# Local attention: one tile's values sent to their key blocks in two column halves instead of at once

## The reference, cut to what matters

```
w = WINDOW                                   # 32
bq = q.reshape(b, h, nw, w, d)               # 16 heads, d = 64
bk2, bv2 = (look(bk), look(bv))              # a block of 32 queries sees its own
                                             # 32 keys and the 32 before them
sim = jnp.einsum('bhwie,bhwje->bhwij', bq, bk2) * QK_SCALE
attn = jax.nn.softmax(sim, -1)
out = jnp.einsum('bhwij,bhwje->bhwie', attn, bv2)
return out.reshape(b, h, n, d)               # then out @ Wo
```

## Time and profile before

| | |
|---|---|
| median of three runs | 5192.34 us |
| the profiled execution: its time | 5198.14 us |
| its span | 5196.3 us, so 1.84 us lie around it |
| busy | PE 4459.6 us (86%), DVE 3876.7 (75%), ACT 3326.2 (64%), POOL 2834.6 (55%) |
| mean granted TensorE clock | 0.934 |
| mean DMA rate | 65 GB/s |
| `f_vw<-f_vt` transfers | 576 of 128 KB and 384 of 64 KB in the `f` stack for lines 833 to 837, as many in `g` |

### The profile page before, as it was taken

How to read it: one execution, slowest core, us unless ns; L and a number is a source line. 1 busy time by engine, 2 the same in 40 slices (tenths; PEclk the granted TensorE clock), 3 DMA queues, 4 the chain that set the end, 5 groups by cost and what they waited for, 6 DMA issues and landing times. The chain is left out here.

```text
span 5196.3 us, 198441 instructions
## 1 busy us (share of the span) xinstructions
PE 4459.6 (86%) x70382; PEld 2776.0 (53%) x70382; DVE 3876.7 (75%) x8099; ACT 3326.2 (64%) x11398; POOL 2834.6 (55%) x2110
## 2 busy tenths in 40 slices
PE   5999999598897988989889756988989889798896
PEld 1333332266565665656656534665656656566565
DVE  7888787387786877868768545877868778687785
ACT  1777777476585775857758413766757667476584
POOL 3000000376675766757667404766757667576674
PEclk6999999899998999999999876999989999899998
DMA  0000000233233232332332302233333322323233
GB/s 13 1 2 2 2 1 1 76 78 86 73 79 87 74 85 76 78 90 73 86 78 78 84 14 86 77 86 78 79 82 79 86 73 77 87 77 85 73 79 97
DMA packets 415347, 340.20 MB, mean 65 GB/s; under 512 B 170607, under 2 KB 312469, under 8 KB 412693
## 3 DMA queue, kind: packets, MB, share of 16 engines
q1 hardware_dynamic: 413972, 332.35, 24.1%
q10 hardware_dynamic: 768, 0.02, 0.0%
HBM read 100.42 MB, written 30.41 MB: 25 GB/s over the span
## 5 line engine op out<-in xcount | busy, mean ns | idle before, releaser
L946 POOL TENSOR_TENSOR g_rn<-g_ss,g_minus_half 128x8 f32<-128x8 f32 x378 | 718.6, 1901 | 394.9 <-DVE g_ss L1151 392.7
L946 POOL TENSOR_TENSOR f_rn<-f_ss,f_minus_half 128x8 f32<-128x8 f32 x378 | 718.3, 1900 | 388.8 <-DVE f_ss L1151 384.3
L427 DVE TENSOR_REDUCE a_maxima<-a_max 128x1 f32<-128x512 f32 x1024 | 651.5, 685 | 150.2 <-PE a_max L541 144.0
L351 ACT ACTIVATE a_pex<-a_scores 128x512 f32<-128x512 f32 x1024 | 531.9, 607 | 162.9 <-PE a_scores L550 162.9
L1014 ACT ACTIVATE f_ex<-f_bank,f_nmx 128x64 f32<-128x64 f32 x1536 | 461.3, 314 | 137.6 <-DVE f_nmx L1144 136.8
L1014 ACT ACTIVATE g_ex<-g_bank,g_nmx 128x64 f32<-128x64 f32 x1536 | 461.4, 314 | 132.2 <-DVE g_nmx L1144 131.4
L951 POOL TENSOR_TENSOR g_qr<-g_t 128x512 f32<-128x512 f32 x384 | 493.3, 1285 | 11.8 <-DVE g_t L1124 11.8
L951 POOL TENSOR_TENSOR f_qr<-f_t 128x512 f32<-128x512 f32 x384 | 492.1, 1282 | 13.0 <-DVE f_t L1124 13.0
L1254 PE MATMUL g_bank<-g_wqkv,g_xT 128*128 128x512 f32 x744 | 437.5, 673 | 69.5 <-DVE g_qh L1138 49.7
L1254 PE MATMUL f_bank<-f_wqkv,f_xT 128*128 128x512 f32 x744 | 431.9, 665 | 71.9 <-DVE f_qh L1138 51.8
L282 POOL COPY a_v_head<-a_v_all 128x128 f32 (+1 forms) x16 | 4.6, 289 | 697.9 <-PE a_sums L559 697.9
(11 more groups left out here) (252 smaller groups left out, 11214.6 us busy)
## 6 DMA issues: line engine op xcount, KB each, us to landing
f_vw<-f_vt SPq DMA_DIRECT2D x576, 128.0 KB
g_vw<-g_vt SPq DMA_DIRECT2D x576, 128.0 KB
f_vw<-f_vt SPq DMA_DIRECT2D x384, 64.0 KB
g_vw<-g_vt SPq DMA_DIRECT2D x384, 64.0 KB
f_wqkv<-in_f_Wqkv_dram SPq DMA_DIRECT2D x7, 1536.0 KB, 8.1
g_wqkv<-in_f_Wqkv_dram SPq DMA_DIRECT2D x7, 1536.0 KB, 7.8
f_xs<-xf SPq DMA_DIRECT2D x196, 32.0 KB, 1.8
g_xs<-xf SPq DMA_DIRECT2D x196, 32.0 KB, 1.8
```

The source lines that it names most:

```text
L351: act.activation(pex[:, kt % 2, i % NG, :], ps_s[i % 3][:], ACT.Exp).then_inc(act_ex, 1)
L427: dve.tensor_reduce(maxima[:, m // 4, m % 4:m % 4 + 1], ps_max[m % 3][:], AX.X, ALU.max).then_inc(dv_max, 1)
L946: pool.tensor_tensor(rn[:, b, :], ss[:, b, :], minus_half[:], ALU.pow).then_inc(pl_rn, 1)
```

## The change

The ten transfers of a tile become twenty, each of half the columns (256 instead of 512 in every row), in two halves h = 0 and 1. The first ten wait for the first copy of the values and for the sums of groups 0 and 1 that last read the buffer, the last ten for the second copy and groups 2 and 3. Each half has a semaphore of its own; ACT's copy c waits for half c of the tile before, and PE's sums wait for half 0 at group 0 and for half 1 at group 2.

```diff
-        ld_vw = [sem(f"ld_vw{p}", 160 * NT // 2, 160) for p in range(2)]
+        ld_vw = [[sem(f"ld_vw{p}{h}", 160 * NT // 2, 160) for h in range(2)] for p in range(2)]
...
-                    sp.wait_ge(act_v, upto(act_v, L, 2 * t - 1)).then_inc(own["sp"], 1)
-                    sp.wait_ge(pe_o, upto(pe_o, L, 4 * t - 9))
                     p = 1 - q
-                    for jj in range(2):
-                        k, cols = KEYS * jj, slice(512 * jj, 512 * jj + 512)
-                        last, mine = (k, k + WINDOW) if p else (k + BLK, k)
-                        sp.dma_start(vw[last:last + WINDOW, p, 0, :], vt[P - WINDOW:P, 1 - p, cols]).then_inc(ld_vw[p], 16)
-                        sp.dma_start(vw[mine:mine + BLK, p, 0, :], vt[0:BLK, p, cols]).then_inc(ld_vw[p], 16)
-                        for blk in range(1, NB):
-                            r = BLK * blk - WINDOW
-                            sp.dma_start(vw[k:k + KEYS, p, blk, :], vt[r:r + KEYS, p, cols]).then_inc(ld_vw[p], 16)
+                    for h in range(2):
+                        sp.wait_ge(act_v, upto(act_v, L, 2 * t - 2 + h)).then_inc(own["sp"], 1)
+                        sp.wait_ge(pe_o, upto(pe_o, L, 4 * t - 11 + 2 * h))
+                        to = slice(256 * h, 256 * h + 256)
+                        for jj in range(2):
+                            k, cols = KEYS * jj, slice(512 * jj + 256 * h, 512 * jj + 256 * h + 256)
+                            last, mine = (k, k + WINDOW) if p else (k + BLK, k)
+                            sp.dma_start(vw[last:last + WINDOW, p, 0, to], vt[P - WINDOW:P, 1 - p, cols]).then_inc(ld_vw[p][h], 16)
+                            sp.dma_start(vw[mine:mine + BLK, p, 0, to], vt[0:BLK, p, cols]).then_inc(ld_vw[p][h], 16)
+                            for blk in range(1, NB):
+                                r = BLK * blk - WINDOW
+                                sp.dma_start(vw[k:k + KEYS, p, blk, to], vt[r:r + KEYS, p, cols]).then_inc(ld_vw[p][h], 16)
...
-                        act.wait_ge(ld_vw[1 - q], upto(ld_vw[1 - q], L, (t - 1) >> 1, 160))
+                        act.wait_ge(ld_vw[1 - q][c], upto(ld_vw[1 - q][c], L, (t - 1) >> 1, 160))
...
-                        if g == 0:
-                            pe.wait_ge(ld_vw[p], upto(ld_vw[p], L, tj >> 1, 160))
+                        if g % 2 == 0:
+                            pe.wait_ge(ld_vw[p][g // 2], upto(ld_vw[p][g // 2], L, tj >> 1, 160))
```

More of the change, by code:

```diff
@@ L799, in _ @@
         def _(sp):
-            for s in (st_a, st_f, ld_vw[0], ld_vw[1]):
+            for s in (st_a, st_f, *ld_vw[0], *ld_vw[1]):
                 sp.sem_inc(s, ahead[s.num])
```

## The result

The changed kernel takes 5329.67 us (median of four runs, 5324.98 to 5344.12); beside it on the same chip the kernel before takes 5193.44 (four runs, 5176.46 to 5194.83). The ratio is 1.0275, with an interval of 1.0246 to 1.0304: slower by 136 us. The forecast had the sign and not the size: 5222, and its range ended at 5285. The two profiled executions lie 131 us apart in span (5327.4 against 5196.3), and the mean granted TensorE clock is 0.926 after and 0.934 before.

What follows compares the result with a forecast made beforehand. The loop was taken to go by the round POOL `rn`, DVE `qh`, maxima, sums of squares; with the change SP becomes the slower. A net 2.5 us a layer, 30 us in twelve, gave 5222 us; range 5145 to 5285.

Steps and rivals of the forecast that it cites:

- The price of an issue: SP's transfers of the values: a half-size one costs the full 0.63 us of spacing, twenty 12.62 us.
- The waits between the halves: SP's queue, ahead of the second half: one wait row and a register operation, 0.28 us of 0.78 a tile.
- SP's sum of 16.46 us a tile: SP in the loop: 12.62 + 3.06 + 0.78 us against a tile of 15.89, so SP is slower by 0.57.
- The excess of the five longer bursts: SP's bursts from 1373 to 1575, marked by instruction-queue packets: 5.8 us over 6.31 each, expected to grow by 2.0.
- The rival in which nothing replaces the waits: SP's half-size issue is cheap, under 0.58 us; the full 85 us are gained, 5107 us; chance 0.07.
- the weighing against the Trainium skill: SP's issue cost: the page alone makes doubling nearly free; the trace differs, ten issues taking 6.31 us.
- The wait that takes the place of the old: ACT's wait in the loop moves from c = 0 to c = 1, 0.3 to 0.8 us a tile, PE's transpose behind it.
- The forecast's last sign: In the changed profile, tiles at the ends of a layer are shorter than now; no size given.
- The loop's waits of before cost nothing, those at the ends do: ACT's waits before c = 0: up to 0.75 us each is free; four at the ends lose 7.1 us a layer.
- Where SP is late: Layer's head, tile 2: second half starts at 1373.0 instead of 1372.47; from there SP finds no gate closed.
- the chain: SP from 1373.0 to tile 15's copy of c = 1: 209.0 us, plus 1.6 and 2.0; +2.7 a layer, taken as 2.5.
- A cover: Slack behind later loads such as `xr`'s, costed at nothing; if one fails, it costs its lateness, 2 us a layer.

## Why the prediction was right in direction and wrong in size

**The price of an issue: right.** The forecast took the full 0.63 us of spacing for a half; the medians are 593, 591 and 597 ns. The waits between the halves: right, 0.31 us for 0.28. SP's sum of 16.46 us a tile: right, 16.42 and 16.51 in the rows above. (The excess of the five longer bursts, 5.8 us in the forecast, comes to 6.4 when their rows are added up.) The rival in which nothing replaces the waits needed an issue under 0.58 us and is out. On the weighing against the Trainium skill ("DMA: Bandwidth & Descriptors", "Issuing engines are not separate DMA queues"): the measurement decides against reading its "usually small relative to the DMA itself" as nearly free, since doubling the issues at equal bytes made SP the bound; its advice to coalesce small transfers ("Rules for kernel authors") agrees with the +2.75%.

**The wait that takes the place of the old: right in the loop.** From the loop's second round on the wait at c = 0 is gone and one of 0.3 to 0.9 us, in the mean of the twelve layers, is there at c = 1, with PE's transpose behind it. In a layer's first tiles it is not: tile 1 waits at c = 0 as well, 3.30 us in the rows below. The forecast's last sign, shorter tiles at both ends of a layer, came out at the far end; the head as a whole is longer.

**The loop's waits of before cost nothing, those at the ends do: right, the size a little low.** The kernel with ten transfers and the last rows first has no waits for transfers left, its loop is not shorter, and it gains 8.5 us a layer where the forecast had 7.1.

**The step that failed: "Where SP is late".** It began the chain at tile 2, with the second half at 1373.0. SP is late from tile 0. ACT's first copies of this layer in the changed kernel, the first of tile 0 and the two of tile 1:

```profile
1344.81 0.59 ACT L1043 COPY f_vt<-f_bank 128x512 f32<-128x512 f32 x1
...
1361.59 0.59 ACT L1043 COPY f_vt<-f_bank 128x512 f32<-128x512 f32 x1 [3.30 <-DMA f_vw<-f_vt]
...
1367.60 0.59 ACT L1043 COPY f_vt<-f_bank 128x512 f32<-128x512 f32 x1 [3.26 <-DMA f_vw<-f_vt]
```

SP's timeline in the same place, from the first weight load to tile 2's second half:

```profile
1338.79 0.37 SPq L813 DMA_DIRECT2D f_w<-in_f_W_dram  x1
...
1347.58 0.40 SPq L878 DMA_DIRECT2D xf<-f_fy  x1
...
1351.07 0.35 SPq L795 DMA_DIRECT2D f_xs<-xf  x1
...
1352.31 0.59 SPq L835 DMA_DIRECT2D f_vw<-f_vt  x1
...
1391.19 0.54 SPq L835 DMA_DIRECT2D f_vw<-f_vt  x1
```

The loads of the next layer's feed-forward weights, the last group's store and the load of `xs` stand ahead of the burst in the queue. The first half's gate opens at 1345.40, when the first copy ends; SP comes to it at 1352.31, 6.9 us late. Across the layers 2 to 6 it is 5.7 to 8.2 us after the copy's start, while in the first layer of a stack, which has no such loads, it is 0.75 us. Not all of it is the loads: between the last group's store and the load of `xs` SP stands for 3.09 us (1347.98 to 1351.07), behind the branch back to the next layer, and the rows name nothing that it waits for. The kernel before stands 0.70 us there in this layer (1337.75 to 1338.45); behind that branch alone it stands 0.2 us in `f`, but 2.5 to 2.9 us in `g`. Before, the late start cost less, for two reasons: the gate was the end of the second copy, which needs some 3 us more, and the burst had half the issues. In the changed kernel the filling tiles have nothing to catch up with. Tile 2's second half starts at 1391.19. The layer's first copy is 9.62 us later than before in this trace (1344.81 against 1335.19), so in the time of before that is 1381.57, 8.6 us after the forecast's 1373.0.

Tile 0 is not the only thing that the start had wrong. Without the reload SP is on time there, and is late again at tile 2: ACT's first copy of tile 2 in the changed kernel without the reload, the starts of SP's two halves for it, and ACT's last copy of the layer.

```profile
1363.22 0.63 ACT L1042 COPY f_vt<-f_bank 128x512 f32<-128x512 f32 x1
```

```profile
1366.76 0.55 SPq L835 DMA_DIRECT2D f_vw<-f_vt  x1
...
1374.28 0.54 SPq L835 DMA_DIRECT2D f_vw<-f_vt  x1
```

```profile
1586.79 0.59 ACT L1042 COPY f_vt<-f_bank 128x512 f32<-128x512 f32 x1 [0.67 <-DMA f_vw<-f_vt]
```

The copy ends at 1363.85 and opens the gate, and the first half starts 2.9 us later, because SP is still at tile 1's twenty transfers and the loads behind them. Three of their rows are longer than elsewhere, by 2.5 us together, and at each of the three the instruction queue moves a packet. The second half starts 40.1 us after the layer's first copy (1374.28 less 1334.19) where the forecast had 37.8 (1373.0 less 1335.19): 2.3 us of the 8.6 are there without the reload.

The rest of the chain was sized right. From that half to the copy of c = 1 in tile 15 the forecast has 209.0 plus 1.6 plus 2.0, 212.6 us; ACT's timeline of the changed kernel has that copy here:

```profile
1603.00 0.59 ACT L1043 COPY f_vt<-f_bank 128x512 f32<-128x512 f32 x1 [1.53 <-DMA f_vw<-f_vt]
```

1603.00 less 1391.19 is 211.8 us. Without the reload it is 212.5 us (1586.79 less 1374.28). A correct chain was hung on a wrong start. In this layer the last copy comes 10.5 us later than before (1603.00 less 9.62 against 1582.89) where the forecast had 2.7, and the difference is the 8.6 us of the start less the 0.8 us that the chain is shorter.

**How the size comes apart.** Measured are 10.8 us a layer where the forecast had 2.5. The table gives the parts. Without the reload the changed kernel's attention takes 252.4 us, 4.0 more than before's 248.4; so with SP on time at tile 0 the forecast would have been 1.5 us too low. In the first layer of the `f` stack of the changed kernel itself, where nothing stands ahead of SP, the last copy is 4.75 us later than before, which agrees. With the reload it is 257.6: another 5.2 us, and that is the failed step, 62 us in twelve layers. Single layers scatter by as much: over the ten that have the loads ahead the two kernels differ by 5.6 us, and of the two first layers, which have none, one differs by 5.9 and the other by -0.7. The kernel before has a part of this lateness too: the same edit takes 2.7 us a layer off its attention (248.4 to 245.7; rather too much, since that profiled execution, 5143.58 us, is the fastest of its nine), which is why the change's own share of it comes to no more than the 41 to 50 us above.

The last 1.6 us a layer are in the tail. A cover failed there that the forecast costed at nothing, that of `xr`'s load ("waited for in c = 3 by DVE, ten us later"; it put a failed cover at 2 us a layer). DVE's wait at the end of this layer, and the load in SP's timeline:

```profile
1631.43 0.29 DVE L1157 TENSOR_TENSOR f_xr<-f_bank,f_xr 128x128 f32<-128x128 f32 x1 [2.92 <-DMA f_xr<-xf]
```

```profile
1623.88 0.35 SPq L854 DMA_DIRECT2D f_xr<-xf  x1
```

DVE goes on 7.55 us after the load's start. The median of these loads lands after 1.8 us, but this one is issued 1.1 us behind the next layer's weights for the projection, 1536 KB, which take 8.8 us in the median; that the one holds up the other is argued from these times. Before, the same load started at 1598.63 and DVE needed it at 1609.08, which was enough.

The wait is shown in seven places, 18.6 us in all, near the tail's growth of some 20 us, but the single tails don't bear it out as the cause. Here are three tails of the changed kernel, from the last copy of a layer to the first of the next: length, PE's busy time, granted clock, DMA share and GB/s.

```profile
1603.00:1683.86 80.86, 63.99 (x806) 0.91 0.34 92
...
3857.46:3935.72 78.26, 60.52 (x807) 0.98 0.35 95
4192.96:4280.62 87.66, 69.21 (x807) 0.84 0.31 85
```

The first two have the wait, of 2.9 and 3.6 us, and are shorter than before's mean of 81.8; the third has none and is among the longest. The tail's length goes with the clock that TensorE is granted in it, and the ten tails of the changed kernel lie between 78.3 and 88.3 us, where before they lie between 80.4 and 84.6. Two means of ten such tails that differ by 1.6 us are hardly clear of each other, and the cause of the 1.6 stays open. It isn't an effect of the weights' loads alone, since without them the tail is as long (83.6 us).

Twelve times 2.5, 5.2, 1.5 and 1.6 us are 130 us. The 1.5 are tile 1's part of the wrong start: over layers 2 to 6 without the reload, tile 2's second half starts 39.8 us after the layer's first copy in the mean, 1.9 later than forecast, and the chain behind it takes 212.2 us, 0.4 less.

## What to carry to other kernels

Before splitting transfers that an ordered queue issues, count issues times the time of one against the tile's time, and look for the number at which the queue has no slack left: here nothing in the loop moves up to eighteen transfers, and twenty cost 2.75%. Start the chain of such a queue at the stage's first item, with all that stands ahead of it in the queue, not where the first visible wait is. And before sending data earlier, ask which of the transfers the waiter really needs: two of ten, sent first with a semaphore of their own, gave the whole prize (-1.8%) with no transfer more.

## What the runs showed of the hardware

An SBUF-to-SBUF transfer costs SP 0.59 us, for 32 or 64 rows and for rows of 1 or 2 KB, four shapes from 32 to 128 KB; the weights' load and the store of the earlier trace rows, with one side in DRAM, 0.33 and 0.36 us in the median. The forecast priced it so and held a lower price at half length for possible. What I had not expected is how sharp the threshold is: fifteen and eighteen transfers have the same loop tile (15.87 and 15.88 us) though eighteen leave only 0.40 us in some tiles between `xr`'s load and the next burst, and twenty have 16.41. Behind the branch back to the next layer SP stands for 2.6 to 3.0 us in ten places of the changed kernel; the kernel before does so in five, and stands 0.2 us in the five others.
